# Key and query numbers of an attention layer as rows in two parts, in a four-layer graph network on one core

## The chip, the cores and the metric

The kernel runs on one core of one Trainium2 chip. Its time is the device time of one execution in microseconds (us), the median of several. A core has five engines that work side by side, each through its own queue in a fixed order: TensorE (PE) multiplies matrices, VectorE (DVE), ScalarE (ACT) and GpSimd (POOL) work on elements, SyncE (SP) issues transfers. They wait for each other by semaphores: an instruction that waits holds up all that stands behind it in its queue.

## The reference, cut to what matters

For each of 16 graphs (512 nodes, 128 numbers per node) four layers follow one another, each on `relu(layernorm(x))`, each with a residual. Layer 0 is where the numbers of the change are used:

```python
feat_proj = (feats @ fc_w + fc_b)            # 8 heads of 128
q = feat_proj @ q_w + q_b                    # one number per node and head
k = feat_proj @ k_w + k_b
logits = q + swapaxes(k, -1, -2)             # 512 x 512 per head
attn = softmax(leaky_relu(logits + (1 - adj) * NEG))
out = sigmoid((attn @ feat_proj).reshape(...) @ fp_w + fp_b + feats)
```

Layer 1 is an attention by `h A h'` with a gate, layer 2 five steps of aggregation and a GRU cell, layer 3 a convolution of 17 taps, distance weights and one more GRU cell.

## The kernel before, in words

Two slots hold two graphs at a time; buffers end in 0 or 1. While graph g goes through softmax (ACT, DVE, POOL) the graph before it goes through layers 2 and 3 (mostly PE), so PE has work of two graphs mixed together. Who comes when is not found by the hardware but written down: every engine's work is cut into steps of strands (`values`, `keys`, `heads`, `layer1`, ...), a table `TURN` gives each step a time and `START` one to each graph, and `in_order` issues the steps by that sum. Changing the numbers changes the fixed order of a queue, and nothing else.

Matrices with full precision are kept as a high and a low part (type fp32r): `mm3` (lines 508, 509, 512) adds high x high, low x high and high x low. Where a weight of 128 x 128 meets 512 columns, this is three instructions.

The places of the change. `values` on PE (line 586 and around) turns the normalized rows of a graph over (`transpose_in`, line 562), then takes 16 numbers per node, the 8 query and 8 key numbers, by 12 products of 16 columns with `VQH` and `VQL` (bank 3), and then eight times `mm3` for the heads' values (the first of each 12 with the weight `M`). Ahead of the 12 stand five products whose result nobody reads (line 586). DVE adds the biases (`QK`, line 1171) and scales (`QN`, line 1174). `keys` on PE (line 619) needs the key numbers of one head as a row repeated on all 128 partitions: four transposes of a broadcast column of `QK`. DVE's masking (line 1201) adds adjacency, ACT exponentiates (lines 908 and 914) with its sums in `den`, DVE inverts them (`rden`, line 1213), POOL scales (line 445), PE turns tiles over (line 638) and multiplies them with the values (line 644), DVE and ACT copying the turned tiles (lines 1223 and 926).

In the same stretch DVE serves layer 1 of the other graph: dots for the gate (line 1256), the new `X` (line 1312), its statistics (lines 1118 to 1126), `AN` from the adjacency (line 1320), and the normalized rows `hN` (line 1132), which PE turns over before layer 2 begins (line 562, then `HT`, line 728, and the aggregation, lines 741 and 745). A GRU cell ends with DVE's lines 1350 and 1352; `accY` is the one of layer 3. Layer 1's sum over neighbours is line 711, the end of a graph on PE line 569.

Of the kernel before, what the change touches and what calls it, by code (L numbers as in the profile page):

```python
# [28 lines left out]
for _name, _width in WIDTHS:  # L29
# [7 lines left out]
AUG = 32 * (BLOCKS - 1) + ROWS5  # L37

# [4 lines left out]
        "bse", "scm", "scs", "hcm", "hcs", "hbm", "hbs", "bmsg"] + ["nq%d" % c for c in range(AUG)] + ["gw%d" % c for c in range(2 * DIM)])  # L43
# [10 lines left out]
    "mask0": 1, "qk_banked": 1, "qk": 1, "g_banked": 8, "g_act": 4, "g_dve": 4,  # L54
# [28 lines left out]
START = (0.000, 130.369, 260.718, 391.050, 521.380, 651.749, 782.086, 912.423, 1042.760,  # L83
          1173.097, 1303.435, 1433.772, 1564.109, 1694.446, 1824.783, 1955.120)
# [3 lines left out]
    ("SP", "transfers"): (3515.678, 3562.397, 3562.397, 3575.622, 3634.067, 3711.988),  # L88
    ("Pool", "inputs"): (3230.966, 3241.946, 3349.882),
    ("Pool", "normalized"): (3291.779, 3291.779, 3291.779, 3291.779, 3291.779, 3291.779, 3293.808, 3298.303,  # L90
# [31 lines left out]
    ("Activation", "values"): (3320.761, 3330.097, 3334.275, 3344.175, 3345.848),  # L122
# [61 lines left out]
def build(nc, x, adj, adjt, nmask, c2w, wraw, prew, fcw, fpw, cols_d, out):  # L184
    with ExitStack() as ctx:
# [7 lines left out]

        WH = sb("WH", [P, WALL], F32R)
        WLO = sb("WLO", [P, WALL], F32R)
        VQH = sb("VQH", [P, 2 * HEADS], F32R)
        VQL = sb("VQL", [P, 2 * HEADS], F32R)
        VQ = sb("VQ", [P, 2 * HEADS])
        CQ = sb("CQ", [P, 2 * HEADS])
# [300 lines left out]
        def _(pe):  # L500
# [71 lines left out]
            def values(g):  # L572
# [930 lines left out]
```

## Time and profile before

| what | us |
|---|---|
| median of 3 runs | 2175.18 |
| lowest and highest run | 2172.43, 2176.92 |
| the profiled execution | 2177.26 |
| its span, first to last instruction | 2175.2 |
| PE busy | 2061.6 (95%) |
| DVE, ACT, POOL busy | 1609.2, 1517.9, 777.0 |

The profile is of one execution; about 2.1 us lie outside its span. A PE instruction's shown duration includes its way through the array: the next starts before it ends. How long one holds the engine is therefore read from one start to the next. TensorE's clock has two levels, 1.2 and 2.4 GHz; PEclk 1.00 in a row means 2.4 GHz throughout, 0.50 means 1.2 GHz throughout.

### The profile page before, as it was taken

The numbers are of one execution on the slowest core, as the hardware profiler recorded it, in microseconds if no ns is written. First come the engines' busy times: TensorE is split into PE (matmuls) and PEld (weight loads), VectorE is DVE, ScalarE is ACT, GpSimd is POOL, SyncE is SP. The second block draws the span as 40 slices with busy tenths as digits, with TensorE's granted clock in tenths as the row PEclk, the third lists the DMA queues.
The fourth block names the chain that finished last, engine by engine and source line by source line (L and its number), as shares of the span: only waits on it lengthen the run. The fifth ranks groups of instructions, "written<-read, shape, count | busy, mean of one in ns | idle before, by whom it ended". The sixth has DMA issues, their size and how long they took to land. (4 is left out here: it accounts for less than half of the span.)

```text
span 2175.2 us, 36465 instructions
## 1 busy us (share of the span) xinstructions
PE 2061.6 (95%) x12700; PEld 1748.4 (80%) x12700; DVE 1609.2 (74%) x4782; ACT 1517.9 (70%) x2968; POOL 777.0 (36%) x888
## 2 busy tenths in 40 slices
PE   7799999999999999999999999999999999999876
PEld 6678797887978878797887979888797888879754
DVE  5687887868778687887868778686877868788643
ACT  5677594967849677694967859587694967859432
POOL 2334334242423433333343433434243342433311
PEclk9999999999999999999999999999999999999988
DMA  3101001010100101001010100101001010100100
GB/s 120 49 20 45 25 1 44 26 45 25 45 25 2 44 25 45 25 2 50 19 45 25 45 25 2 44 25 45 25 28 42 1 44 25 45 6 1 49 0 5
DMA packets 47319, 65.73 MB, mean 30 GB/s; under 512 B 3744, under 2 KB 21536, under 8 KB 47008
## 3 DMA queue, kind: packets, MB, share of 16 engines
q1 hardware_dynamic: 47136, 63.41, 8.9%
q8 instruction: 100, 1.64, 0.3%
q14 instruction: 83, 0.68, 0.1%
HBM read 59.21 MB, written 4.19 MB: 29 GB/s over the span
## 5 line engine op out<-in xcount | busy, mean ns | idle before, releaser
L644 PE MATMUL banks<-F,PT 128*128 128x128 f32 x4096 | 543.3, 276 | 2.3 <-DVE PT L1223 1.5
L644 PEld LDWEIGHTS banks<-F,PT 128*128 128x128 f32 x4096 | 507.1, 192 | 15.2 <-DVE PT L1223 2.0
L478 POOL TENSOR_TENSOR HS<-HT,HS 128x512 fp32r<-128x512 f32 x64 | 83.4, 1304 | 539.4 <-ACT HS L990 539.4
L1223 DVE COPY PT<-banks 128x512 f32<-128x512 f32 x256 | 175.7, 686 | 116.2 <-PE banks L638 115.5
L926 ACT ACTIVATE PT<-banks 128x512 f32<-128x512 f32 x256 | 151.2, 591 | 89.0 <-PE banks L638 87.1
L961 ACT ACTIVATE F<-banks,dcols 128x512 f32<-128x512 f32 x288 | 193.6, 684 | 23.3 <-PE banks L512 19.1
L445 POOL TENSOR_SCALAR tiles<-tiles,rden 128x512 f32<-128x512 f32 x192 | 143.7, 763 | 97.1 <-DVE rden L1213 96.9
L415 POOL TENSOR_TENSOR rstd<-var,mhalf 128x4 f32<-128x4 f32 x64 | 72.4, 1131 | 271.4 <-DVE var L1126 271.4
L508 PE MATMUL banks<-HS,WH 128*128 128x512 f32 (+1 forms) x368 | 157.9, 429 | 1.6 <-ACT HS L889 1.4
L445 POOL TENSOR_SCALAR U<-U,rden 128x512 f32<-128x512 f32 x192 | 130.5, 699 | 72.7 <-DVE rden L1213 72.5
L509 PE MATMUL banks<-HS,WLO 128*128 128x512 f32 (+1 forms) x368 | 147.5, 401 | 0.0
L914 ACT ACTIVATE tiles<-tiles 128x512 f32<-128x512 f32 x192 | 138.5, 721 | 9.1
L914 ACT ACTIVATE U<-U 128x512 f32<-128x512 f32 x192 | 138.6, 722 | 5.4 <-DVE rden L1213 0.4
L445 POOL TENSOR_SCALAR adjT<-adjT,rden 128x512 f32<-128x512 f32 x128 | 88.2, 699 | 140.8 <-DVE rden L1213 140.7
L908 ACT ACTIVATE U<-U,QN 128x513 f32<-128x513 f32 x192 | 137.3, 715 | 1.4 <-DVE U L1201 1.4
L908 ACT ACTIVATE tiles<-tiles,QN 128x513 f32<-128x513 f32 x192 | 137.5, 716 | 0.0
L508 PE MATMUL banks<-R,WH 128*128 128x512 f32 x336 | 135.2, 402 | 1.4 <-DVE R L1412 1.4
L509 PE MATMUL banks<-R,WLO 128*128 128x512 f32 x336 | 133.1, 396 | 0.0
L512 PE MATMUL banks<-R,WH 128*128 128x512 f32 x336 | 132.0, 400 | 0.0
L512 PE MATMUL banks<-HS,WH 128*128 128x512 f32 (+1 forms) x368 | 129.6, 401 | 0.0
L1201 DVE CUSTOM_DVE_ANT_0 U<-adjN,banks 128x512 f32<-128x512 f32 x192 | 124.4, 679 | 0.6 <-issue 0.6
L1201 DVE CUSTOM_DVE_ANT_0 tiles<-adjN,banks 128x512 f32<-128x512 f32 x192 | 124.4, 679 | 0.0
(216 smaller groups left out, 5309.3 us busy)
## 6 DMA issues: line engine op xcount, KB each, us to landing
adjN<-in_adj_dram SPq DMA_DIRECT2D x32, 1024.0 KB, 5.6
adjT<-in_adjt_dram SPq DMA_DIRECT2D x16, 1024.0 KB, 5.7
xin<-in_x_dram SPq DMA_DIRECT2D x18, 256.0 KB, 2.9
out_dram<-X SPq DMA_DIRECT2D x16, 256.0 KB, 6.0
F<-in_wraw_dram SPq DMA_DIRECT2D x1, 1076.0 KB, 9.6
adjT<-in_c2w_dram SPq DMA_DIRECT2D x1, 1024.0 KB, 11.1
PT<-in_fcw_dram SPq DMA_DIRECT2D x1, 512.0 KB, 5.2
PT<-in_fpw_dram SPq DMA_DIRECT2D x1, 512.0 KB, 6.8
```

Source lines behind the costliest of these rows:

```text
L445: pool.tensor_scalar(SC[s][h % RING][:, t, 0:NODES], SC[s][h % RING][:, t, 0:NODES], rden[s][:, t:t + 1], 1.0, ALU.mult, ALU.mult).then_in ...
L478: pool.tensor_tensor(HL[s], HT[s][:, :], HH[s].bitcast(F32), ALU.subtract).then_inc(S["h_new_low"], 1)
L508: pe.matmul(dst, w[0], xs[0], start=start, stop=False)
L509: pe.matmul(dst, w[1], xs[0], start=False, stop=False)
L512: return pe.matmul(dst, w[0], xs[1], start=False, stop=stop)
L644: last = pe.matmul(B[s][:, 3, part(j)], PT[s][:, k, part(j)], G[s][:, k, h * DIM:(h + 1) * DIM], start=(h == 0 and j == 0 and k == 0), sto ...
L908: act.activation(SC[s][h % RING][:, t, :], SC[s][h % RING][:, t, :], ACT.Prelu, bias=QN[s][:, t, h:h + 1], scale=0.01, alpha=100.0).then_i ...
L914: act.activation(SC[s][h % RING][:, t, 0:NODES], SC[s][h % RING][:, t, 0:NODES], ACT.Exp, bias=SC[s][h % RING][:, t, NODES:NODES + 1], sca ...
L926: act.activation(PT[s][:, j, :], pt_bank(s, j), ACT.Copy).then_inc(S["pt_act"], 1)
L961: act.activation(F[s][:, tile, :], B[s][:, bank, :], func, bias=dcol(bias), scale=0.5)\
L1201: dve.tensor_tensor_reduce(out=SC[s][h % RING][:, t, 0:NODES], in0=adjN[s][:, t, :], in1=B[s][:, 0, :], scale=1.0, scalar=3.0e38, op0=ALU. ...
L1223: dve.tensor_copy(PT[s][:, j, :], pt_bank(s, j)).then_inc(S["pt_dve"], 1)
```

## The change

The query and key numbers are computed the other way round: the stationary side is now `VQH` and `VQL` with 104 columns, so that three products of 512 columns give rows (partitions 0 to 7 and 32 to 39 the keys, 64 to 71 and 96 to 103 the queries, each twice). ACT writes the high part of one copy (`KS`, for the other copy zero, by a scale column of 0 or 1), DVE subtracts it from the bank: `KR` then holds high and low part of each row, as fp32r, in partitions of their own. One product of a column of `pick` (0 and 1) broadcast to 128 columns with `KR` adds both parts and puts one head's key row on all partitions; four small products with `pick` give back the query numbers per node. `den` and `rden` get three sets. Waits that others imply are dropped. Five unread products become 17, in another place, for every graph but the first; there are 18 in the first graph's layer 1, and, for the last graph only, 26, five times 10, 13 and 13. The bias row `ob` is computed earlier at the start. `START` and the whole of `TURN` are other numbers.

```diff
-START = (0.000, 130.369, 260.718, 391.050, 521.380, ...
+START = (0.000, 131.658, 263.298, 394.959, 526.603, ...
-    ("PE", "keys"): (3288.100, 3289.199, 3290.522, 3298.667, 3321.282, 3343.182, 3360.968, 3375.271),
+    ("PE", "keys"): (166.698, 169.779, 177.359, 190.668, 191.962, 214.493, 223.487, 236.182),
...
+        KS = [U[s][0:ROWSQ, TILES - 1, :].bitcast(F32R) for s in SL]
-        den = [sb(f"den{s}", [P, TILES]) for s in SL]
+        den = [sb(f"den{s}", [P, RING, TILES]) for s in SL]
...
-                pe.matmul(B[1][:, 3, 0:HEADS], dcol("qkw").broadcast_to([P, P]), cols[:, 0:HEADS]).then_inc(vq_banked, 1)
+                pe.matmul(B[1][:, 3, 0:HEADS], dcol("qkw").broadcast_to([P, P]), cols[:, 0:HEADS])
+                for h in range(HEADS):
+                    pe.matmul(B[1][:, 3, P:2 * P], cols[:, h:h + 1].broadcast_to([P, P]), fp[:, part(h)], start=(h == 0), stop=False)
+                pe.matmul(B[1][:, 3, P:2 * P], col("fpb").broadcast_to([P, P]), ident[:, :], start=False, stop=True)\
+                    .then_inc(vq_banked, 1)
...
+            def busy(bank, n):
+                for k in range(n):
+                    pe.matmul(bank, WH[:, 0:P], WH[:, 0:4 * P])
...
-                if g >= SLOTS:
-                    for k in range(5):
-                        pe.matmul(B[s][:, 3, :], WH[:, 0:P], WH[:, 0:4 * P])
-                pe.wait_ge(*own("h_low", g, 0))
                 if g == 0:
                     pe.wait_ge(vq_low, 1)
-                for t in range(TILES):
-                    last = mm3(B[s][:, 3, 16 * t:16 * t + 16], (HH[s][:, part(t)], HL[s][:, part(t)]),
-                               (VQH[:, :], VQL[:, :]))
+                pe.wait_ge(*own("h_high", g, 0))
+                high(B[s][0:ROWSQ, 3, :], (VQH[:, :], VQL[:, :]), (HH[s], HL[s]))
+                pe.wait_ge(*own("h_low", g, 0))
+                low(B[s][0:ROWSQ, 3, :], (VQH[:, :], VQL[:, :]), (HH[s], HL[s])).then_inc(S["kq_banked"], 1)
+                yield
+                if g >= 1:
+                    busy(B[s][:, 0, :], 17)
+                pe.wait_ge(*after("kq_rows", g))
+                for t in range(TILES):
+                    last = pe.matmul(B[s][:, 0, HEADS * t:HEADS * (t + 1)], KR[s][64:ROWSQ, part(t)], pick[64:ROWSQ, :])
                 last.then_inc(S["qk_banked"], 1)
...
-                    if i == 2:
-                        pe.wait_ge(*after("qk", g))
...
-                    for t in range(TILES):
-                        last = pe.transpose(B[s][:, 0, part(t)],
-                                            QK[s][:, t, HEADS + h:HEADS + h + 1].broadcast_to([P, P]), ident[:, :])
-                    last.then_inc(S["kb_banked"], 1)
+                    pe.matmul(B[s][:, 0, :], pick[0:32 + HEADS, h:h + 1].broadcast_to([32 + HEADS, P]),
+                              KR[s][0:32 + HEADS, :]).then_inc(S["kb_banked"], 1)
...
+                    busy(B[s][:, 1, :], 18)
...
+                if g == GRAPHS - 1:
+                    busy(B[s][:, 1, :], 26)
...
+                        if g == GRAPHS - 1:
+                            pe.wait_ge(*after("r", cell - 1))
+                            busy(B[s][:, 2, :], 10)
...
+                if g == GRAPHS - 1:
+                    pe.wait_ge(*after("c2_scaled", g))
+                    busy(B[s][:, 3, :], 13)
                 pe.wait_ge(*after("nmp_low", g))
...
+                act.wait_ge(*after("kq_banked", g))
+                act.activation(KS[s], B[s][0:ROWSQ, 3, :], ACT.Identity, bias=0.0, scale=cols[0:ROWSQ, CI["qlow"]:CI["qlow"] + 1])\
+                    .then_inc(S["kq_high"], 1)
...
+                dve.wait_ge(*after("kq_high", g))
+                dve.tensor_tensor(KR[s][:, :], B[s][0:ROWSQ, 3, :], KS[s].bitcast(F32), ALU.subtract).then_inc(S["kq_rows"], 1)
```

Three places show what this does to a queue. In these rows `[waits ...]` names the semaphores, and L numbers are the lines of the kernel that the rows belong to (before: 569 graph's end, 586 unread products; after: 572 the same end, 558 unread products, 598 the query numbers).

PE before, where a graph ends (`accY`) and the values of the next in that slot begin:

```order
L569 MATMUL banks0<-ident,accY0 128x128 [waits h_new]
L569 MATMUL banks0<-ident,accY0 128x128 x3
L586 MATMUL banks0<-WH 128x512 [waits hn]
L586 MATMUL banks0<-WH 128x512 x4
L508 MATMUL banks0<-VQH,HS0 128x16 [waits h_low_0]
L509 MATMUL banks0<-VQH,HS0 128x16
L512 MATMUL banks0<-VQL,HS0 128x16
```

PE after, the same place:

```order
L508 MATMUL banks0<-HS0,VQH 104x512 [waits h_high_0,hn]
L509 MATMUL banks0<-HS0,VQL 104x512
L512 MATMUL banks0<-HS0,VQH 104x512 [waits h_low_0]
L572 MATMUL banks0<-ident,accY0 128x128 [waits h_new]
L572 MATMUL banks0<-ident,accY0 128x128 x3
L558 MATMUL banks0<-WH 128x512 x17
L598 MATMUL banks0<-pick,KR0 128x8 [waits kq_rows]
L598 MATMUL banks0<-pick,KR0 128x8 x3
L508 MATMUL banks0<-WH,HS0 128x512 [waits h_new]
```

The three row products moved ahead of the graph's end, and all value products now stand behind `kq_rows`.

DVE before, serving this place (slot 1 begins, slot 0 ends its layer 1; `var`, `AN`, `hN` belong to layer 1 and 2):

```order
L1126 TENSOR_SCALAR var0<-mv0 128x4 [waits aggregated_0]
L1171 TENSOR_TENSOR QK1<-banks1,CQ 128x64 [waits qk_banked]
L1174 TENSOR_SCALAR QN1<-QK1 128x32 [waits qk]
L1320 TENSOR_SCALAR AN0<-adjN0 128x2048 [waits hp_banked,adjN_loaded0]
L1132 TENSOR_SCALAR hN0<-X0,mv0,rstd0 128x128 [waits rstd_0]
L1132 TENSOR_SCALAR hN0<-X0,mv0,rstd0 128x128 x3
```

DVE after (1192 is the new subtraction, 1169 the residual that before stood ahead of the gate dots):

```order
L1138 TENSOR_SCALAR var0<-mv0 128x4 [waits aggregated_0]
L1192 TENSOR_TENSOR KR1<-banks1,U1 104x512 [waits kq_high]
L1169 TENSOR_TENSOR X1<-banks1,X1 128x512 [waits y_banked_1]
L1335 TENSOR_SCALAR AN0<-adjN0 128x2048 [waits hp_banked,adjN_loaded0]
L1144 TENSOR_SCALAR hN0<-X0,mv0,rstd0 128x128 [waits rstd_0]
L1144 TENSOR_SCALAR hN0<-X0,mv0,rstd0 128x128 x3
L1195 TENSOR_TENSOR QK1<-banks1,CQ 128x32 [waits qk_banked]
```

`KR` took the place of `QK`, which moved behind `hN`; the residual moved from ahead of the gate to here.

PE after, between two cells of the last graph's layer 2 (before, the transposes of line 728 followed the last product at once):

```order
L512 MATMUL banks1<-R1,WH 128x512
L558 MATMUL banks1<-WH 128x512 [waits r]
L558 MATMUL banks1<-WH 128x512 x9
L730 MATMUL banks1<-ident,HT1 128x128 [waits h_new]
L730 MATMUL banks1<-ident,HT1 128x128 x3
```

Ten unread products now stand in what was a bare wait for `h_new`.

## Rows read from the trace of the kernel before

**Rows 1.** Page, part 1: busy time, share, instructions
```profile
PE 2061.6 (95%) x12700; PEld 1748.4 (80%) x12700; DVE 1609.2 (74%) x4782; ACT 1517.9 (70%) x2968; POOL 777.0 (36%) x888
```

**Rows 2.** Timeline of DVE: start us, us, engine, line, what; one QK per graph
```profile
20.99 0.22 DVE L1171 TENSOR_TENSOR QK<-banks,CQ 128x64 f32<-128x64 f32 x1 [0.76 <-PE banks L512]
...
119.14 0.22 DVE L1171 TENSOR_TENSOR QK<-banks,CQ 128x64 f32<-128x64 f32 x1
...
1935.85 0.22 DVE L1171 TENSOR_TENSOR QK<-banks,CQ 128x64 f32<-128x64 f32 x1
```

**Rows 3.** Waits of PE from 249 to 1936 us: total us, times, longest
```profile
PE banks L508 <- DVE QK L1171: 21.3, 13, 1.9
PE banks L728 <- ACT HT L954: 8.5, 13, 0.7
PE banks L569 <- DVE accY L1352: 3.3, 13, 0.3
...
PE banks L728 <- DVE HT L1352: 1.4, 7, 0.5
```

**Rows 4.** Timeline of PE: two products of 512 columns, then two groups of transposes
```profile
909.63 0.39 PE L508 MATMUL banks<-WH,HS 128*128 128x512 f32 x1
909.86 0.39 PE L509 MATMUL banks<-WH,HS 128*128 128x512 f32 x1
...
952.86 0.60 PE L619 MATMUL banks<-ident,QK 128*128 128x128 f32 x4
953.30 0.60 PE L638 MATMUL banks<-ident,U 128*128 128x128 f32 x4
```

**Rows 5.** Timeline of PE where one graph ends and the next begins
```profile
1022.16 0.66 PE L569 MATMUL banks<-ident,accY 128*128 128x128 f32 x4 [0.26 <-DVE accY L1352]
1022.57 1.40 PE L586 MATMUL banks<-WH 128*128 128x512 f32 x5
1024.20 0.28 PE L508 MATMUL banks<-VQH,HS 128*128 128x16 f32 x1 [0.23 <-DVE HS L1138]
...
1028.81 0.50 PE L508 MATMUL banks<-WH,HS 128*128 128x512 f32 x1 [1.63 <-DVE QK L1171]
...
1032.36 0.66 PE L728 MATMUL banks<-ident,HT 128*128 128x128 f32 x4 [0.69 <-ACT HT L954]
```

**Rows 6.** Timeline of DVE in the same stretch
```profile
1021.41 0.69 DVE L1352 SCALAR_TENSOR_TENSOR accY<-F 128x512 f32<-128x512 f32 x1
1022.85 0.69 DVE L1157 TENSOR_TENSOR X<-banks,X 128x512 f32<-128x512 f32 x1 [0.75 <-PE banks L569]
1023.46 0.68 DVE L1138 SCALAR_TENSOR_TENSOR HS<-banks,HS 128x512 fp32r<-128x512 f32 x1
...
1028.45 0.17 DVE L1126 TENSOR_SCALAR var<-mv 128x4 f32<-128x4 f32 x1
...
1028.88 1.22 DVE L1320 TENSOR_SCALAR AN<-adjN 128x2048 fp32r<-128x2048 f32 x1
1030.17 1.11 DVE L1132 TENSOR_SCALAR hN<-X,mv,rstd 128x128 f32<-128x128 f32 x4
```

**Rows 7.** Stretches: us, busy PE, PEld, DVE, ACT, POOL, clock, DMA share, GB/s
```profile
249.30:378.90 129.60, 126.63 (x790) 107.81 (x790) 99.76 (x298) 94.26 (x185) 48.46 (x55) 1.00 0.09 29
...
2080.90:2091.30 10.40, 7.02 (x30) 5.15 (x30) 5.09 (x9) 4.50 (x7) 1.30 (x1) 1.00 0.01 2
...
2115.00:2127.60 12.60, 9.20 (x30) 7.06 (x30) 5.09 (x8) 4.50 (x7) 1.29 (x1) 0.77 0.00 0
2127.60:2145.00 17.40, 12.07 (x40) 8.38 (x40) 5.08 (x22) 3.77 (x6) 2.98 (x3) 0.62 0.00 1
```

**Rows 8.** Timeline of PE with the last graph alone
```profile
2080.99 0.66 PE L728 MATMUL banks<-ident,HT 128*128 128x128 f32 x4 [3.37 <-DVE HT L1352]
...
2135.47 0.63 PE L509 MATMUL banks<-HS,WLO 128*128 128x512 f32 x1
2135.90 0.63 PE L508 MATMUL banks<-HS,WH 128*128 128x512 f32 x1
```

More of the change, by code:

```diff
@@ L42 @@
         "bih3r", "bih3z", "bih3n", "bhh3r", "bhh3z", "bhh3n",
-        "bse", "scm", "scs", "hcm", "hcs", "hbm", "hbs", "bmsg"] + ["nq%d" % c for c in range(AUG)] + ["gw%d" % c for c in range(2 * DIM)])
+        "qlow", "bse", "scm", "scs", "hcm", "hcs", "hbm", "hbs", "bmsg"] + ["nq%d" % c for c in range(AUG)] + ["gw%d" % c for c in range(2 * DIM)] + ["pk%d" % h for h in range(HEADS)])
 CI = {n: i for i, n in enumerate(COLS)}
@@ new lines @@
+    ("SP", "transfers"): (0.000, 6.720, 28.455, 31.853, 211.238, 217.728),
+    ("Pool", "inputs"): (63.748, 71.077, 175.343),
+    ("Pool", "normalized"): (137.764, 137.764, 140.756, 140.756, 145.791, 145.958, 146.520, 146.641, 148.247,
[26 rows of a table added]
+    ("Activation", "values"): (280.268, 283.534, 283.534, 289.782, 308.796, 312.315),
+    ("Activation", "weights"): (281.986, 281.986, 287.195, 307.884, 309.784),
+    ("Activation", "softmax"): (294.464, 295.181, 295.181, 298.237, 303.387, 309.676, 309.676, 311.233, 311.233,
[5 rows of a table added]
@@ new lines @@
+    ("Activation", "tile_copies"): (314.345, 318.415, 328.588, 332.960, 346.050, 351.163, 352.673, 357.805, 362.988,
[9 rows of a table added]
+    ("DVE", "values"): (291.932, 299.290, 303.284, 311.648, 312.505, 316.050, 316.827, 319.568, 320.672, 321.279),
+    ("DVE", "weights"): (300.169, 306.745, 311.878, 313.915, 313.915, 320.273, 320.273, 351.308),
+    ("DVE", "softmax"): (317.554, 317.711, 318.421, 318.503, 320.486, 321.059, 321.500, 321.500, 330.265, 330.265,
+        338.773, 343.405, 359.012, 367.293, 367.342, 367.342, 379.728, 381.734, 387.576, 390.185, 391.958, 392.222,
+        393.928, 394.317, 398.780, 401.731, 404.237, 404.237, 415.564, 421.165, 423.967, 424.135),
@@ L234, in build @@
         HT = [sb(f"HT{s}", [P, NODES]) for s in SL]
-        hN = [sb(f"hN{s}", [P, NODES]) for s in SL]
+        hN, KR = [], []
+        for s in SL:
+            with nc.sbuf_tensor(f"hN{s}", [P, NODES], F32) as t:
+                hN.append(t)
+            KR.append(sb(f"KR{s}", [ROWSQ, NODES], F32R))
         X = [sb(f"X{s}", [P, TILES, DIM]) for s in SL]
@@ L238, in build @@
         nm = [sb(f"nm{s}", [P, TILES]) for s in SL]
-        QK = [sb(f"QK{s}", [P, TILES, 2 * HEADS]) for s in SL]
+        QK = [sb(f"QK{s}", [P, TILES, HEADS]) for s in SL]
         QN = [sb(f"QN{s}", [P, TILES, HEADS]) for s in SL]
@@ L536, in weights @@
                 last.then_inc(m_banked, 1)
-                yield
-                pe.wait_ge(vq_ready, 1)
-                for h in range(HEADS):
-                    pe.matmul(B[1][:, 3, 0:DIM], cols[:, h:h + 1].broadcast_to([P, P]), fp[:, part(h)], start=(h == 0), stop=False)
-                pe.matmul(B[1][:, 3, 0:DIM], col("fpb").broadcast_to([P, P]), ident[:, :], start=False, stop=True)\
-                    .then_inc(m_banked, 1)
                 yield
@@ L666, in scores @@
                     if t == 0:
-                        pe.wait_ge(*after("t1_high", g))
                         pe.wait_ge(*after("h1_high", g))
@@ L707, in layer1 @@
                     yield
-                    pe.wait_ge(*after("h1_scaled", g, t + 1))
+                    if t % 2 == 0:
+                        pe.wait_ge(*after("h1_scaled", g, t + 1))
                     pe.wait_ge(*attended(g, t))
@@ L738, in layer2 @@
                     pe.wait_ge(*after("rows_high", turn))
-                    pe.wait_ge(*after("adjacency", g))
+                    if layer == 0:
+                        pe.wait_ge(*after("adjacency", g))
                     for t in range(TILES):
@@ L772, in layer3 @@
                 yield
+                if g == GRAPHS - 1:
+                    pe.wait_ge(*after("r", cell - 1))
+                    busy(B[s][:, 2, :], 10)
                 pe.wait_ge(*after("h_new", cell - 1))
@@ L775, in layer3 @@
                 yield
+                if g == GRAPHS - 1:
+                    busy(B[s][:, 2, :], 13)
                 transpose_in(g, 3)
@@ L778, in layer3 @@
                 pe.wait_ge(*own("h_high", g, 3))
-                pe.wait_ge(*own("residual", g, 2))
                 high(B[s][:, 1, :], W("c1"), (HH[s], HL[s]))
@@ L1072, in weights @@
                 vq = B[1][:, 2, 0:2 * HEADS].rearrange("p (h a) -> p a h", a=2)
[L1073 to L1075 removed]
+                dve.tensor_scalar(CQ[:, :], B[1][:, 3, 0:HEADS], d2("tq"), None, ALU.add)
+                for a in (0, 32):
+                    dve.tensor_scalar(VQ[:, a:a + HEADS], vq[:, 1, :], -1.0, None, ALU.mult)
+                dve.tensor_copy(pick[:, :], cols[0:ROWSQ, CI["pk0"]:CI["pk0"] + HEADS])
+                for a in (64, 96):
+                    last = dve.tensor_copy(VQ[:, a:a + HEADS], vq[:, 0, :])
+                last.then_inc(vq_ready, 1)
+                dve.tensor_copy(ob[:, :], B[1][:, 3, P:2 * P]).then_inc(ob_ready, 1)
                 yield
@@ L1210, in denominators @@
                         dve.wait_ge(*after("exped", g * HEADS + h, t + 1))
-                        if h >= 1:
-                            dve.wait_ge(*after("attn", g * HEADS + h - 1, t + 1))
-                        dve.reciprocal(rden[s][:, t:t + 1], den[s][:, t:t + 1]).then_inc(S["rden"], 1)
+                        dve.reciprocal(rden[s][:, h % RING, t:t + 1], den[s][:, h % RING, t:t + 1]).then_inc(S["rden"], 1)
             def tile_copies(g):
@@ L1327, in cand_a @@
                 s = g % SLOTS
-                dve.wait_ge(*after("hn", cell))
-                dve.wait_ge(*after("r", cell))
+                dve.wait_ge(*after("r" if cell % (LAYERS2 + 1) < LAYERS2 else "hn", cell))
                 dve.scalar_tensor_tensor(F[s][:, 3, :], F[s][:, 0, :], 1.0, F[s][:, 2, :], ALU.add, ALU.mult)\
@@ L1472, in rows @@
         return _np.array(values, _np.float32)
-    none = rows(0, 0, 0, 0, 0)
+    none, heads_one = rows(0, 0, 0, 0, 0), _np.ones(HEADS, _np.float32)
     moving, still = rows(1, 1, 1, 0, 1), rows(2, 2, 2, 1, 0)
     moving_one, still_one = rows(0, 0, 0, -1, 0), rows(0, 0, 0, 0, -1)
-    nq = _np.zeros((P, AUG), _np.float32)
+    nq, pick = _np.zeros((P, AUG), _np.float32), _np.tile(_np.eye(32, HEADS, dtype=_np.float32), (4, 1))
     for b in range(BLOCKS):
```

107 lines of the change are left out of this document (43 added, 64 removed), and 102 rows, old and new, of the table TURN.

## The prediction, made before the changed kernel ran

> **What bounds the kernel now.** I read the busy times first: PE is busy for 2061.6 us of 2175.2 [rows 1], everything else much less. Then the rhythm: DVE's `QK` comes once per graph, from 119.14 to 1935.85 in 14 equal steps of 129.8 us [rows 2], so those 1817 us are one pattern; before it stand 21 us of setup and 98 us with one graph, behind it 239 us in which the last graph ends up alone. In a steady step the clock is 1.00 and PE is idle for about 3 of 129.6 us [rows 7]. The list of waits says where: `QK` 21.3 us in 13 graphs (1.6 each), `HT` from ACT 8.5, `accY` 3.3, and `HT` from DVE 1.4 [rows 3]. The first three are one place, the border between two graphs [rows 5]. Outside it PE hardly waits, so there a product taken off PE is time gained, and a product put on is time lost; at the border the chain through DVE decides. The last 115 us are different: PE waits 3.4 us in each cell [rows 8], and the granted clock falls.
>
> **The keys of a head.** One product of 512 columns holds PE for 0.23 us (909.63 to 909.86), a group of four transposes for 0.44 (952.86 to 953.30) [rows 4]. The change puts one of the former for one of the latter, eight times a graph, which is 0.21 us each. The first is part of the border, below. The second stands right ahead of a cell's `HT`, for which PE already waits in 7 of 13 graphs [rows 3], so what it frees is waited away. Six remain: 6 x 0.21 = 1.27 us a graph. The product has 40 rows and a broadcast weight, a form that no row shows. Bounds: as dear as four transposes (0) and, with all eight counted, 1.7 us. I take 1.27, since its 512 columns are those of the neighbouring products.
>
> **The border, PE's work.** Twelve small products go (about 0.11 each, the rate of the transposes: 1.3 us), and five unread ones (1.2 us). Three row products (0.7), four small ones (0.4) and 17 unread ones (17 x 0.23 = 3.95 us) come. Together with the keys that is 6.1 us off PE (with all 32 transposes) and 7.0 us on: PE's total work per graph grows by 0.9 us. Whether the kernel gets faster hangs on the 3.95 us lying inside a wait.
>
> **The border, the chain.** I walk it on the clock of [rows 5, 6]. `accY` is ready at about 22.1 (times less 1000). Before: DVE idles until PE has turned it over, adds the residual at 22.85, and starts `HS` at 23.46; `var` starts 5.0 us later at 28.45, then `QK`, `AN` at 28.88, `hN` at 30.17, ready at 31.28, and PE begins with `HT` 1.1 us after that at 32.36. After: `HS` is next to `accY` and starts at 22.1; the same run of gate, `X` and statistics is then over at 27.2; `KR` (one more pass of 512, 0.61 as between 22.85 and 23.46) to 27.85; the residual, moved here, to 28.45; `AN` 1.3 to 29.75; `hN` ready at 30.8. So `HT` on PE starts at 31.9 instead of 32.36. ACT has one extra copy to `KS` ahead and one copy of a value more between `HT` and the rows of the cell, so of these 0.45 us I keep 0.3.
> On PE: the third row product waits for `HS` until 22.8, and ends at 23.05; the transposes of `accY` end at 23.5, the 17 unread products at 27.4. `KR` is there at 27.9. They lie inside the wait, with 0.5 us left bare. Then four small products to 28.35, nine value products to 30.45, and PE waits again for `hN` at 30.8. What lies behind `KR` on PE, all value products of the graph, has the slack of that last wait (0.35 us) and no more. What hides the 17 products is DVE's gate and statistics of the other graph; if that cover went, each would cost 0.23 us. Bounds of the border: 1.0 us gained (if all waits but `hN`'s closed) and 2.8 us lost (twelve more unread products wholly on top). I take 0.3 gained, as the walk uses durations of the very same instructions.
>
> **The new order.** Nearly all steps got other times. I compared the queues of PE, DVE and ACT over one graph. Between a cell's last product and the next cell's transposes there stands as much softmax work as before or more, and a row of masks ahead of a cell's subtraction is matched by PE work put in the same gap. The cover over layer 1's normalization and over layer 3's `nmp_low` is thinner, by about 1 us and 0.3 us, but by the durations still enough. I take off 0.06 for this. Dropped waits and the three sets of `den` cost and give nothing where PE is the bound: they are implied by others, and ACT is 27% idle [rows 7].
> Per graph: 1.27 + 0.3 - 0.06 = 1.5 us. Fourteen steps [rows 2]: 21.0 us. The last graph's softmax, beside the layers of the one before, has the same keys again: 1.3.
>
> **The end.** From 2067 us on one graph runs alone. A cell at clock 1.00 takes 10.40 us, one at 0.77 takes 12.60, though all instructions are the same [rows 7]. A product of 512 columns holds PE for 0.43 us at the lower level (2135.47 to 2135.90) [rows 8] instead of 0.23. Three of the four cells behind the first are slow, the longest by 2.2 us, which bounds them at 6.6; the start of layer 3 runs at 0.62 [rows 7], and nine such products and eight transposes there, at most twice as long, give 3 us more; some 0.5 more at the very end. The change fills these waits: ten unread products are 2.3 us in a wait of 3.4 plus the products' tail [rows 8], 26 are 6.1 us ahead of `hN`, where PE idles for some 7. If that holds the level at 2.4 GHz, up to 10 us come back. I take 8; bounds 0 and 10. They cost something where they outlast the wait: the last 13 hold PE for 3.0 us, and the row they stand before is ready earlier than that, which I put at 0.3 within the 8. Should all of them run at the lower level, 26 x 0.43 = 11.2 us, and up to 4 us would be lost there.
>
> **The start.** `QK` of the first graph comes at 20.99 [rows 2]. Ahead of it now lie an ACT pass, a DVE pass and the bias products, some 3 us by the same lengths. Against that, ACT, which bounds the first graph's softmax, gets the big conversion of weights before it instead of within it, and 18 unread products should keep the clock up in layer 1. I take 1 us gained, between 3 lost and 3 gained.
>
> **The sum.** 21.0 + 1.3 + 8 + 1 = 31.3 us off the profiled execution of 2177.3 (span 2175.2) is 2146.0. That execution is 2.1 above the median of the runs, so the forecast is 2143.9 us.
>
> **Rivals.**
> *The unread products lie on top* (slower). Suppose rows, gate and statistics don't stretch over the 17 products, or the new order leaves as much waiting as there was: 129.6 us a graph plus the 0.9 of work. Then 14 x 0.9 = 12.6 and 0.8 for the last softmax are lost; with 9 gained at both ends it ends at 2179.6 from a base of 2175.2, and with the ends at zero at 2189. It decides from about 2.1 us more idle time a graph than I found. For it: PE's work does grow, and every value product now depends on one row of DVE that has a long queue ahead. Against it: the walk above, on DVE's own rows [rows 6].
> *The clock at the end does not hold.* Then the 8 are missing: 2152. Speaking for it: waits of more than 1 us remain in each cell even with ten products in them. Against: in the steady stretch waits of 1.6 and 0.7 us leave it at 1.00 [rows 5, 7]. The Trainium skill, "TensorE: Matmul & The Clock Gate", section "A second HAM failure mode: psum-queue depth-cycling", says that frequent short idles between groups of products can make the clock swing between its levels; by that rule this rival holds, and the steady stretch here speaks against it.
> *The key product is no cheaper* than four transposes (the change doesn't do what it says): 1.27 x 14 + 1.3 = 19 us less gain, 2163.
> *The order is better than I can see*: PE's remaining waits close as well, 1.3 us a graph more, 2125.
>
> **Chances.** Forecast 0.56; clock 0.12, 2152; key product 0.08, 2163; on top 0.17, 2180; better order 0.07, 2125. The range runs from 2127 to 2176: it takes in the bounds of the border and the keys except for the far end of the slower rival and half of the best. A change of 0.2% (4.35 us) is about what a measurement of this kernel can tell from none, so faster is below 2170.8, slower above 2179.5. All cases but the slower rival are faster, which gives 0.80 with a rest for their tails; the rival straddles the upper bound: same 0.09, slower 0.11.
>
> **What would show each step.** In the new profile: steps between two `QK` of 128.3 us; the key product 0.23 us from its start to the next; the 17 products followed by a wait of about 0.5 us for `KR`; `HT` on PE about 9.8 us after `accY` instead of 10.2; no new entry of over 0.3 us a graph in the list of PE's waits; cells of the last graph near 10.4 us at clock 1.00. A step of 130.5 us would be the slower rival. I would be wrong most easily in the new order: a wait for `weights3`, `normed` or `masked` in the middle of a graph, which the queues alone don't show, would cost its length 14 times.

## The result: slower by 42 us, and the profile after

The changed kernel takes 2217.1 us (median of 4 runs, 2213.2 to 2219.3), the kernel before 2174.7 in the same company: a ratio of 1.0192, 95% interval 1.0179 to 1.0204. The forecast was 2143.9. The profiled execution of the changed kernel is one of 2213.2 us (span 2211.4); the forecast for such a one was 2146.0, so 67 us are to be explained.

The rhythm tells most of it. These are the first two and the last `QK` on DVE, from the order of time of the changed kernel (columns: start, duration, engine, line, operation, output<-input, shape):

```profile
25.22 0.18 DVE L1195 TENSOR_TENSOR QK<-banks,CQ 128x32 f32<-128x32 f32 x1
...
127.08 0.18 DVE L1195 TENSOR_TENSOR QK<-banks,CQ 128x32 f32<-128x32 f32 x1
...
1980.17 0.18 DVE L1195 TENSOR_TENSOR QK<-banks,CQ 128x32 f32<-128x32 f32 x1
```

The 14 steps behind 127.08 are 132.36 us long, 2.6 more than in [rows 2] and 4.1 more than forecast: 57 of the 67 us. The second `QK` comes 7.9 us later than before, where 1 us earlier was forecast: 9 more. Behind the last one the kernel takes 231.2 us instead of 239.4, 8.2 less, where 9.3 was forecast.

The list of PE's waits in the steady stretch, 260 to 1975 us, has become shorter than [rows 3]:

```profile
PE banks L598 <- DVE KR L1192: 17.9, 12, 1.5
PE banks L572 <- DVE accY L1366: 2.8, 11, 0.3
PE banks L508 <- DVE X L1169: 1.9, 1, 1.9
PE banks L512 <- DVE HS L1150: 0.8, 2, 0.4
```

About 1.9 us a graph instead of 2.9, all at the border. So in each graph PE is busy for 3.6 us more than before, where the forecast has 0.9 more work. A busy PE is not PE at its peak: what is missing stands in the distances from start to start. Two places show it. The first is a key product between two groups of transposes and value products, PE in the order of time:

```profile
443.45 0.60 PE L636 MATMUL banks<-ident,U 128*128 128x128 f32 x4
443.98 0.50 PE L622 MATMUL banks<-KR,pick 40*128 40x512 f32 x1
444.41 1.16 PE L642 MATMUL banks<-F,PT 128*128 128x128 f32 x8
445.40 0.60 PE L636 MATMUL banks<-ident,U 128*128 128x128 f32 x4
```

Four transposes hold PE until 443.98, which is 0.53 instead of the 0.44 of [rows 4]; the key product 0.43 instead of 0.23; the eight value products behind it 0.99 instead of 0.89. From 443.45 to 445.40 are 1.95 us. In the kernel before the same stretch, with four transposes for the key product, took 0.44 + 0.44 + 0.89 = 1.77. The product of 512 columns is dearer than the four transposes, by 0.18 us. It is not the product alone (0.43 against their 0.44): its neighbours are held longer too.

The second place is the border between two graphs, here one with its clock below it (columns of the windows: the stretch, its length, busy us and number of PE, PEld, DVE, ACT, POOL, then the granted clock, DMA share, GB/s):

```profile
647.09 0.60 PE L572 MATMUL banks<-ident,accY 128*128 128x128 f32 x4
647.45 4.13 PE L558 MATMUL banks<-WH 128*128 128x512 f32 x17
652.92 0.60 PE L598 MATMUL banks<-pick,KR 40*128 40x8 f32 x4 [1.35 <-DVE KR L1192]
...
654.00 0.63 PE L509 MATMUL banks<-WH,HS 128*128 128x512 f32 x1
654.43 0.63 PE L512 MATMUL banks<-WLO,HS 128*128 128x512 f32 x1
...
656.98 0.40 PE L512 MATMUL banks<-WLO,HS 128*128 128x512 f32 x1
657.21 0.60 PE L565 MATMUL banks<-ident,hN 128*128 128x128 f32 x4
```

```profile
649.00:652.90 3.90, 2.57 (x12) 1.80 (x10) 3.69 (x17) 0.82 (x2) 0.55 (x1) 1.00 0.00 0
...
654.00:657.00 3.00, 3.00 (x9) 2.32 (x8) 2.53 (x8) 0.60 (x1) 0.00 (x0) 0.51 0.39 85
657.00:660.00 3.00, 3.00 (x17) 2.24 (x16) 1.69 (x7) 2.12 (x4) 0.00 (x0) 1.00 0.97 317
```

Behind the 17 unread products PE stands still for 1.35 us, not the 0.5 of the forecast, and then the granted clock is 0.51, the level of 1.2 GHz: the value products are 0.43 us apart instead of 0.23. This happens at 9 of the 14 borders. By the granted clock of the trace, TensorE is at the lower level for 35 us of the 14 steps, all of it at borders, against 7 us in the kernel before.

Why `KR` is late stands on DVE. The same border one graph earlier, DVE and the one pass of POOL that falls in it:

```profile
514.21 0.69 DVE L1366 SCALAR_TENSOR_TENSOR accY<-F 128x512 f32<-128x512 f32 x1
514.82 0.68 DVE L1150 SCALAR_TENSOR_TENSOR HS<-banks,HS 128x512 fp32r<-128x512 f32 x1
515.42 0.28 DVE L1271 CUSTOM_DVE_ANT_0 F<-F,cols 128x128 f32<-128x128 f32 x1
...
515.62 1.37 DVE L1271 CUSTOM_DVE_ANT_0 F<-F,cols 128x128 f32<-128x128 f32 x1
...
516.93 0.28 DVE L1271 CUSTOM_DVE_ANT_0 F<-F,cols 128x128 f32<-128x128 f32 x1
...
520.98 0.68 DVE L1192 TENSOR_TENSOR KR<-banks,U 104x512 fp32r<-104x512 f32 x1
```

```profile
515.47 1.37 POOL L469 TENSOR_TENSOR F<-F 128x512 f32<-128x512 f32 x1 [5.50 <-ACT F L958]
```

One of the four gate sums (the dots for the gate) takes 1.37 us; its sisters take 0.28. It ends 0.1 us after POOL's pass. This is so at each of the 14 borders. In [rows 6] `HS` stood behind the residual, 1.4 us later, and the gate sums began at 1024.06, when POOL's pass was over. In the kernel before that pass is this one:

```profile
1022.68 1.30 POOL L469 TENSOR_TENSOR F<-F 128x512 f32<-128x512 f32 x1 [5.06 <-ACT F L948]
```

One border of the 14, called the odd one below, is unlike the others, and unlike the queues shown ahead of the prediction: there the residual (L1169) stands on DVE behind `AN` and `hN` instead of ahead of them. Their due times in `TURN` are 578.279 and 446.661, 131.618 apart; the starts of neighbouring graphs are 131.640 or more apart, but for one pair with 131.611, and there the order turns round. PE's value products wait for it; that is the one wait of 1.9 us for `X` in the list above.

### The profile page after: what moved, and what is told of

Same layout as the page of the kernel before. It is cut to its first block and busy times, and to the rows that moved or that the text cites. A ratio compares the mean times of both kernels' runs of the same rounds, so it can differ in the third digit from the quotient of the medians.

```text
span 2211.4 us, 34516 instructions
## 1 busy us (share of the span) xinstructions
PE 2140.0 (97%) x12541; PEld 1768.7 (80%) x12541; DVE 1641.2 (74%) x4801; ACT 1511.3 (68%) x2984; POOL 798.8 (36%) x888
## 5 line engine op out<-in xcount | busy, mean ns | idle before, releaser
L445 POOL TENSOR_SCALAR U<-U,rden 128x512 f32<-128x512 f32 x192 | 140.4, 743 | 369.7 <-DVE rden L1230 368.6
L936 ACT ACTIVATE PT<-banks 128x512 f32<-128x512 f32 x256 | 150.6, 588 | 96.8 <-PE banks L636 96.4
L445 POOL TENSOR_SCALAR tiles<-tiles,rden 128x512 f32<-128x512 f32 x192 | 138.0, 726 | 90.7 <-DVE rden L1230 89.3
L508 PE MATMUL banks<-HS,WH 128*128 128x512 f32 (+1 forms) x368 | 155.3, 422 | 1.4 <-ACT HS L899 1.4
L445 POOL TENSOR_SCALAR adjT<-adjT,rden 128x512 f32<-128x512 f32 x128 | 93.5, 741 | 127.5 <-DVE rden L1230 127.5
L512 PE MATMUL banks<-HS,WH 128*128 128x512 f32 (+1 forms) x368 | 127.5, 396 | 0.0
```

Source lines behind the costliest of these rows:

```text
L445: pool.tensor_scalar(SC[s][h % RING][:, t, 0:NODES], SC[s][h % RING][:, t, 0:NODES], rden[s][:, h % RING, t:t + 1], 1.0, ALU.mult, ALU.mul ...
L508: pe.matmul(dst, w[0], xs[0], start=start, stop=False)
L512: return pe.matmul(dst, w[0], xs[1], start=False, stop=stop)
L936: act.activation(PT[s][:, j, :], pt_bank(s, j), ACT.Copy).then_inc(S["pt_act"], 1)
```

## The experiments

Each has the changed kernel as its base unless it says otherwise. "Step" is the mean of the 14 steps between `QK`s; the ratios are to the kernel before on the same chip. The last column is the time in these 14 steps for which the granted clock is at 1.2 GHz, idle time of PE included.

| kernel | us | ratio, 95% interval | step | us at 1.2 GHz in 14 steps |
|---|---|---|---|---|
| before | 2174.7 | 1 | 129.8 | 7 |
| changed | 2217.1 | 1.0192 (1.0179 to 1.0204) | 132.4 | 35 |
| e1_wide | 2173.4 | 0.9993 (0.9984 to 1.0002) | 129.8 | 22 |
| e9_rows64 | 2211.3 | 1.0167 (1.0146 to 1.0189) | 132.3 | 36 |
| e5_free | 2189.8 | 1.0067 (1.0050 to 1.0084) | 130.8 | 3 |
| e2_busy0 | 2228.4 | 1.0244 (1.0229 to 1.0259) | 133.5 | 101 |
| e8_busy23 | 2198.0 | 1.0113 (1.0094 to 1.0132) | 131.3 | 0 |
| e6_wide_free | 2151.5 | 0.9900 (0.9884 to 0.9916) | 128.6 | 3 |
| e7_kr_first | 2148.9 | 0.9888 (0.9872 to 0.9905) | 128.4 | 0 |
| e12_no13 | 2147.5 | 0.9881 (0.9867 to 0.9896) | 128.5 | 3 |
| e10_an_pool | 2222.3 | 1.0223 (1.0208 to 1.0238) | 133.1 | 61 |
| e11_less | 2223.7 | 1.0233 (1.0216 to 1.0250) | 133.1 | 82 |
| e4_tail (on before) | 2171.7 | 0.9983 (0.9974 to 0.9993) | 129.7 | 3 |
| e13_order (on before) | 2221.0 | 1.0211 (1.0193 to 1.0228) | 132.7 | 89 |

**e1_wide: the rows of the key product.**

```
-pe.matmul(B[s][:, 0, :], pick[0:32 + HEADS, h:h + 1].broadcast_to([32 + HEADS, P]), KR[s][0:32 + HEADS, :])
+pe.matmul(B[s][:, 0, :], pick[:, h:h + 1].broadcast_to([ROWSQ, P]), KR[s][:, :])
```

`pick` gets a second set of columns, for the query products, which take all rows too; the set for the keys is zero in the rows of the queries, and the other way round.

> The changed kernel, with the key product and the four small query products taking all 104 rows of `KR` (the rows that are not wanted meet zeros in `pick`) instead of 40. Theory: the 40-row product holds PE for 0.43 us because of its row count, and what stands next to it is held 0.1 us longer too; with 104 rows it takes 0.23 as its neighbours do. Then a graph's step falls by 8 x 0.2 = 1.6 us, up to 2.0, from 132.4 to about 130.6, and the time from 2217 to about 2193. Rival: the broadcast weights are what costs (or the change between a product of this kind and one of transposes): then it stays at 0.43 and the time at 2217.

The theory held, and more came than the 1.6 to 2.0 us a graph that it asked for: 2.6. The same place in its trace:

```profile
428.59 0.60 PE L636 MATMUL banks<-ident,U 128*128 128x128 f32 x4
428.95 0.48 PE L622 MATMUL banks<-KR,pick 104*128 104x512 f32 x1
429.26 1.05 PE L642 MATMUL banks<-F,PT 128*128 128x128 f32 x8
430.15 0.60 PE L636 MATMUL banks<-ident,U 128*128 128x128 f32 x4
```

0.36, 0.31 and 0.89: 1.56 us, 0.39 less than with 40 rows and 0.21 less than the 1.77 of the transposes, which is the very difference that the forecast took. Eight times 0.39 are 3.1; 2.6 arrive, and a little of these may be clock (22 us at the lower level instead of 35). That the rest is lost in PE's waits at the border is likely and was not taken apart. The broadcast weights are still there, so it isn't they.

**e9_rows64: 64 rows instead of 104.**

```
-pe.matmul(..., pick[:, h:h + 1].broadcast_to([ROWSQ, P]), KR[s][:, :])
+pe.matmul(..., pick[0:64, h:h + 1].broadcast_to([64, P]), KR[s][0:64, :])
```

> As the first experiment (104 rows), but the key product takes 64 rows of `KR`; the query products stay at 104. Tells what it is about the 40 rows. If products with few rows are dear because their rows are not those of the products around them, 64 rows should cost like 40: 0.53, 0.42 and 0.34 us from start to start before, at and behind the key product, and about 2.5 us a graph more than with 104 rows, 2209. If only a count that is no multiple of 32, or one that splits a group of rows, is dear, 64 costs like 104 and the time is 2173.

64 rows cost what 40 do (0.53, 0.42 and 1.00 from start to start in the same kind of place, the median of 28), so it is neither a count that is no multiple of 32 nor one that splits a group. A product that uses half of the rows or fewer, among products that use more, is what is dear, and what stands on either side of it pays too. Tried were 40, 64 and 104 rows. The Trainium skill has a rule that would explain it, "TensorEngine Tiling (Array Packing)", sections "Tiling Modes", "Key Properties" and "When to Use Tiling": arrays of 64 rows, for 64 contraction rows or fewer, are a mode of their own, and changing the mode drains the engine. It presents the mode as something one chooses. That a plain product of few rows falls into it is an inference; no trace shows the mode. The price agrees in kind: 0.39 us for a key product and its two changes.

**e5_free: POOL's pass away from the gate sums.** X = (h - hp) gate + (x + h + hp) is written (h - hp)(gate - 1) + (x + 2h):

```
-pool.wait_ge(*after("hp", g))
-pool.tensor_tensor(F[s][:, 7, :], F[s][:, 6, :], F[s][:, 2, :], ALU.add)
+pool.tensor_tensor(F[s][:, 7, :], F[s][:, 6, :], F[s][:, 5, :], ALU.add)
...
+dve.tensor_scalar(gate[s][:, 0, :], gate[s][:, 0, :], -1.0, None, ALU.add).then_inc(S["gate_less"], 1)
+dve.wait_ge(*after("gate_less", g))
```

> The changed kernel, with X = (h - hp)(gate - 1) + (x + 2h) in place of (h - hp) gate + (x + h + hp): GpSimd's pass that waited for hp now needs only h, and runs some 6 us earlier, away from DVE's gate sums; DVE gets one pass of 4 columns more. Theory: GpSimd's pass and DVE's gate sums hold each other up at the border (one pass of 128 columns takes 1.37 us there and 0.28 elsewhere). Then that pass takes 0.28, `KR` comes 0.9 us earlier, PE's wait for it falls from 1.5 to 0.6, the step by 0.9, and by up to 1.9 if the clock no longer falls behind the wait: 2204 to 2190. Rival: the long pass has another cause: it stays at 1.37 and the time at 2217 or a little above.

Held, at the good end. All four sums now take 0.28, and `KR` comes 5.7 us after the start of `accY` at every border instead of 6.8. Two of the four:

```profile
507.80 0.28 DVE L1270 CUSTOM_DVE_ANT_0 F<-F,cols 128x128 f32<-128x128 f32 x1
...
508.00 0.29 DVE L1270 CUSTOM_DVE_ANT_0 F<-F,cols 128x128 f32<-128x128 f32 x1
```

PE waits 0.5 for `KR` instead of 1.5 (and 0.7 instead of 0.3 for `accY`), and the clock falls at one border only: the odd one, where PE also waits 2.3 us for the residual. 27 us in all.

**e2_busy0 and e8_busy23: the number of unread products at the border.** 0 and 23 instead of 17:

```
-busy(B[s][:, 0, :], 17)
+busy(B[s][:, 0, :], 23)
```

> The changed kernel without the 17 unread products at the border between two graphs. Theory: DVE's chain to `KR` sets the border, the products lie inside PE's wait; then PE waits 5.5 us there instead of 1.5, the step stays at 132.4, and the time within 6 us of 2217 (the clock may fall for longer behind the longer wait: up to 2 us a graph more, 2245). Rival, the one put on record as slower: the products lie on top: then 3.95 us a graph come back, a step of 128.5 and 2162 us.

> The changed kernel with 23 unread products at the border instead of 17. Six more are 1.4 us, which is the wait for `KR` (1.5 us). Theory: the clock falls only because PE stands still there for 1.5 us; with the wait filled it stays at its upper level, the 35 us at the lower level in 14 graphs go, half of them are time: a step about 1.2 us shorter, 2200. Rival: the fall has nothing to do with the wait, or more products outlast it: 2217 or more.

Both theories held. Without the 17, not one of their 3.95 us comes back: PE waits 5.4 us in every graph, and the clock falls in each such wait or right behind it.

```profile
PE banks L596 <- DVE KR L1190: 64.4, 12, 5.4
```

The step becomes 1.1 us longer, not shorter, so the rival of the record, unread products on top, is out. With 23 the wait is closed and the clock stays at its upper level through all 14 steps (columns as in the windows above; the clock is the 1.00):

```profile
124.72:1962.38 1837.66, 1829.29 (x10905) 1519.43 (x10905) 1424.81 (x4173) 1311.83 (x2604) 694.63 (x770) 1.00 0.09 29
```

The step is 1.1 us shorter although PE has 1.4 us more to do. That is the price of the wait of 1.5 us, as clock and not as idle time: 35 us at half speed are at most 17.5 us of work, 1.2 us a graph, and 1.1 come back.

**e6_wide_free: both edits.**

> The changed kernel with both edits: key and query products over 104 rows, and GpSimd's pass no longer behind hp. Theory: the two losses are separate things in separate places, so they add: from a step of 132.4 the 2.6 us of the one and the 1.6 of the other go, 128.2, with at most 0.5 shared, since each of the two has part of its gain from the same low clock behind the wait for `KR`; 2217 - 44 - 27 = 2146, up to 2152. Rival: the border and the keys share one limit (DVE's chain): then the second edit brings less than half of its 27, and the time is over 2160.

They add: 2151.5 us where the sum said 2146 to 2152. The mean step is 128.6, and 12 of the 14 lie within 0.2 of 128.3, which is the forecast's own number. The other two are 129.3 and 131.4, on both sides of the odd border, where PE waits for the residual and the clock falls behind the wait:

```profile
763.61 0.80 PE L507 MATMUL banks<-WH,HS 128*128 128x512 f32 x1 [2.35 <-DVE X L1168]
```

These 4.1 us are the whole difference of 0.3 us a graph. The parts of the forecast that no experiment names apart (the new order elsewhere, the walk along DVE without the stall) so hold as a sum; their errors may cancel, since the keys alone now save 8 x 0.21 = 1.7 us where 1.27 was forecast, and PE waits 0.7 us for `accY` instead of 0.3. The kernel is 1.0% faster than the one before.

**e7_kr_first: `KR` ahead of the statistics.** One due time of the statistics on DVE is raised from 443.857 to 444.500, so that `KR` comes first.

> As the last one, with `KR` on DVE ahead of the statistics instead of behind them. Theory: with the stall gone, `hN` (statistics, reciprocal root on GpSimd, `AN` in between) is what PE waits for last, and `KR` 0.6 us earlier only moves PE's wait from the small query products to the transposes of `hN`: the step stays within 0.2 us, the time within 3 us of the last one. Rival: `KR` sets the border: a step 0.4 to 0.6 us shorter, 6 to 8 us in all.

As expected: PE's wait for `KR` is gone, the transposes of `hN` are now what comes last (four of them take 0.82 us from start to start, each held back a little, instead of 0.35), the step is 0.2 us shorter. In this kernel DVE works without a gap from `accY` to `hN`, so its passes should set the border; the next experiment was to show it and did not get that far.

**e10_an_pool and e11_less: `AN` on POOL, then fewer unread products** (base: e6_wide_free).

```
-dve.tensor_scalar(AN[s][:, :, :], adjN[s][:, :, :], 0.0, None, ALU.not_equal)
+pool.tensor_scalar(AN[s][:, :, :], adjN[s][:, :, :], 0.0, None, ALU.is_gt)
```

> As the kernel with both edits (104 rows, GpSimd's pass freed), and the pass that writes `AN` (2048 columns, 1.1 us of DVE) goes to GpSimd, which is idle there (with `greater than 0` for `not 0`, the same for entries 0 and 1). Theory: with the stall gone DVE works without a gap from `accY` to `hN`, so its passes set the border; 1.1 us fewer give `hN` up to 0.9 us earlier (GpSimd's reciprocal root then comes last), but with 17 unread products PE is behind by itself: some 0.3 to 0.5 us a graph, 2144 to 2147. Rival: GpSimd's long pass and DVE's gate sums hold each other up as the other pass did: one gate pass of 2 us, and 10 us or more lost, 2162.

> As the last one, with 12 unread products at the border instead of 17 (1.17 us less of PE's work). Theory: there the unread products are on top by now; the step falls by up to 0.9 us against the kernel with both edits, 2138. Rival 1: DVE still sets the border: PE waits longer, the time stays within 3 us of the last one. Rival 2 (if GpSimd's pass stalls DVE): within 3 us of the last one too, but with the wait for `KR` of over 2 us in the list.

The rival won by far. POOL needs 5.76 us where DVE took 1.22, and the first gate sum waits for most of it:

```profile
511.12 3.13 DVE L1274 CUSTOM_DVE_ANT_0 F<-F,cols 128x128 f32<-128x128 f32 x1
```

```profile
510.08 5.76 POOL L471 TENSOR_SCALAR AN<-adjN 128x2048 fp32r<-128x2048 f32 x1 [3.22 <-PE banks L711]
```

The next sum starts at 514.18, while POOL's pass ends at 515.84 in the profile, in which the spans of POOL are rough: here DVE seems not to wait for its end, unlike at L469. PE then waits 3.3 us for `KR`. The second kernel lost as much, as its second rival says: less work on PE can't help where DVE is late. Part of the 4.5 us a graph that are lost is the clock again, 61 us at the lower level.

**e13_order: the order alone, on the kernel before.** One due time: the last graph's residual (L1157) moves from between `accY` and `HS` to behind `QK` and `QN`.

> The kernel before with one step of the new order alone: on DVE the last graph's residual no longer stands between `accY` and `HS`, but behind the statistics. Theory: the order alone makes the stall. `HS` comes 1.4 us earlier, the gate sums then fall on GpSimd's pass and one of them takes 1.37 us instead of 0.28; that and the residual behind the statistics eat the gain: `hN` within 0.3 us of where it was, the step within 0.3, the time between 2172 and 2178. Rival: no stall without the rest of the change: `hN` 0.9 us earlier, a step of 128.9, and 2162.

The mechanism held and the time did not: 2221.0, 47 us slower. The stall is there (one gate sum of 1.38 at 1039.70), and `hN` starts 9.0 us after `accY` instead of 8.8. But my expectation left out that PE's second value product waits for this residual, and what the clock makes of that:

```profile
1046.14 0.80 PE L508 MATMUL banks<-WH,HS 128*128 128x512 f32 x1 [3.27 <-DVE X L1157]
1046.73 0.63 PE L509 MATMUL banks<-WH,HS 128*128 128x512 f32 x1
...
1050.15 1.05 PE L619 MATMUL banks<-ident,QK 128*128 128x128 f32 x4
...
1052.74 0.66 PE L728 MATMUL banks<-ident,HT 128*128 128x128 f32 x4 [0.69 <-ACT HT L954]
```

The wait is 3.27 us instead of 1.63 [rows 5] and comes three products earlier. The nine products behind it take 4.0 us, which at 0.23 each would be 2.1, and the transposes behind them twice their time, all on the way to `HT`, which comes 14.5 us after the start of `accY` instead of 10.95. The clock in this stretch:

```profile
1046.10:1050.20 4.10, 4.06 (x10) 3.10 (x11) 2.83 (x6) 0.60 (x1) 1.16 (x1) 0.50 0.39 82
```

Over the 14 steps it is at the lower level for 89 us instead of 7, after each of the 14 waits. One moved step of DVE, 0.61 us long, costs more than the whole change, most of it by way of the clock behind a wait that is 1.6 us longer. It also shows that the stall needs nothing but the order; its own price here stands inside the 47 us and was not taken apart.

**e4_tail and e12_no13: the unread products of the last graph.** The first adds them (26, 10 a cell, 13, 13) to the kernel before. The second takes the last 13 out of e7_kr_first:

```
-if g == GRAPHS - 1:
-    pe.wait_ge(*after("c2_scaled", g))
-    busy(B[s][:, 3, :], 13)
```

> The kernel before, with only the unread products of the last graph added (26 ahead of `hN` in layer 1, 10 in each wait of a cell, 13 and 13 in layer 3). Theory: they hold the clock at its upper level there, which is worth 8 us: 2167. Rival: the part of the changed kernel behind the last `QK` is 8 us shorter for another reason (its keys, its order): 2175.

> As the kernel with `KR` ahead of the statistics, without the 13 unread products ahead of `nmp_low` in the last graph. Theory: they outlast their wait: from the transposes of layer 3 to those of `accY` the last graph takes 28.7 us with them and 27.6 in the kernel before, at the same clock. Without them 1.1 us less, 2148. Rival: they keep the clock up there: without them it falls, and the time is 1 to 3 us longer.

They hold the clock: in e4_tail the granted clock stays at its upper level from 2072.7, in the first cell, until the last 5 us of the kernel, and the cells of the last graph come 10.4 us apart, as the one cell at clock 1.00 did in the kernel before [rows 7]:

```profile
2080.50 0.66 PE L737 MATMUL banks<-ident,HT 128*128 128x128 f32 x4 [1.08 <-DVE HT L1369]
2090.89 0.66 PE L737 MATMUL banks<-ident,HT 128*128 128x128 f32 x4 [1.06 <-DVE HT L1369]
2101.28 0.66 PE L737 MATMUL banks<-ident,HT 128*128 128x128 f32 x4 [1.08 <-DVE HT L1369]
2111.69 0.66 PE L737 MATMUL banks<-ident,HT 128*128 128x128 f32 x4 [1.06 <-DVE HT L1369]
```

But the gain is 3.3 us by the medians (4.6 from the first `HT` of the last graph to its `accY` in the traces), not 8. The last 13 are part of the reason: from the transposes of layer 3 (L790 before, L797 after) to those of `accY` it takes 27.6 us before, 28.7 in the changed kernel and 30.0 in e4_tail. Without them 2147.5 instead of 2148.9; the intervals of the two overlap, so the medians alone don't settle it, and the traces show 27.1 us in that stretch instead of the 28.7 of e7_kr_first: 1.5 less. This is the fastest kernel here, 1.2% ahead of the one before.

## Why the prediction was wrong, step by step

**The keys of a head: the step that failed first.** "I take 1.27, since its 512 columns are those of the neighbouring products": the columns are, the 40 rows are not. The term was bounded by "as dear as four transposes (0)", and the product is dearer than they are: 0.18 us more instead of 0.21 less, eight times a graph. The text had named the form as one that no row shows and then bounded it by rows of other forms, with no room for a loss. e1_wide gives 2.6 us a graph back, and 5.0 us in the first graph, where the next `QK` comes 96.8 us after the first instead of 101.9. In all 42 of the 67 us, profile against profile (44 by the medians). The rival "the key product is no cheaper" (2163) had the place right and ended its price at zero.

**The border, the chain: right walk, one pass overlooked.** The walk used durations of the same instructions and moved them 1.4 us earlier. It didn't ask what other engines do at the new time. POOL's pass behind hp, 1.3 us long, starts 1.3 us after `accY` in both kernels; the gate sums came to lie on it. The forecast has `KR` on DVE 5.8 us after the start of `accY`; it came after 6.8. So the wait of 0.5 us became 1.5. e5_free takes it away. The Trainium skill says it of this pair of engines, "SBUF — State Buffer", section "Who interferes with whom": a DVE instruction with two inputs in SBUF contends with a GpSimd instruction that reads there; one with a single input, outside the modes of DVE that take two ports, does not. The traces agree: the gate sums read `F` and `cols`, and wait; the residual pass of [rows 6], with one input in the banks, ran from 1022.85 beside the same pass of POOL (from 1022.68, 1.30 us) and took its 0.61 us.

**The border, PE's work: right.** The 17 products lie inside the wait, with 1.5 us bare instead of 0.5; nothing comes back without them (e2_busy0).

**What the forecast had no term for: the clock inside the steady stretch.** It cited waits of 1.6 and 0.7 us at clock 1.00 [rows 5, 7] against the rival of the clock at the end, and didn't ask whether a wait behind other neighbours would leave it there. It does not: 1.35 to 1.5 us behind 17 products let it fall in 9 of 14 graphs. The rule of the Trainium skill that is cited there is about frequent short idles between groups of products. The middle has one such wait a graph, so it is hardly that case; the end with its ten products in each cell comes nearer to it, and there the clock stayed up behind waits of 1.1 us. What decides between a fall and none behind 1.5 us, the runs don't show. e8_busy23 prices the falls at 1.1 us a graph; part of what e5_free gains is the same money.

**The new order: right but for one border.** No wait of over 0.3 us a graph appeared in the middle, and e6_wide_free runs at the forecast step. The place at which I said I would most easily be wrong was not the place. The queues were compared over one graph, though, and at one border of the 14 they differ: `X` behind `hN`, 4.1 us in e6_wide_free, 0.3 a graph. `START` and `TURN` alone would have told it.

**The end: right in direction, too high.** 8.2 us came in all where 9.3 was forecast. The cells came out as forecast, 10.4 us at clock 1.00, and that is 5 of the 8; the last 13 products cost 1.1 to 1.5 instead of 0.3. In e4_tail the products alone bring 3.3 to 4.6 us. Where the rest of the 8.2 comes from was not taken apart.

**The start: wrong, by 4 us beside the rows.** `QK` comes at 25.2 instead of 21.0, and of the gain that was set against it nothing shows. (In e2_busy0 and e8_busy23, whose start is the same code, it comes at 23.5 and 23.8, so up to 1.7 us of the 4.2 may belong to this one execution.) The bias products for `ob` now hold PE for 3.6 us (from 12.86) ahead of the product of the weights, where before they came behind it; so ACT's conversion of `WH` begins at 20.14 instead of 16.66. DVE's part of the weights' split waits 1.5 us for that, `KR` (22.34) stands behind it, and the small products wait 2.3 us for `KR`. The better pace after e1_wide pays 1.3 of the 4.2 back. This was read from the trace and not tried.

The sum: 57 us in the steps (2.6 a graph for the rows; 1.2 more that came with POOL's pass and the clock behind the wait; 0.3 from the odd border), 9 at the start (5 of them the rows again), 1 at the end.

## What to carry to other kernels

A product of few rows among products of many was not priced by its columns here: give it the rows of its neighbours, with zeros where it has none, before counting what it saves. When a change moves an engine's passes in time, look at what the other engines do at the new time, above all GpSimd under any pass of DVE with two inputs in SBUF. And of a wait on PE ask not only how long it is but what stands behind it: products at half the clock on the chain can cost more than the wait, and filling it with unread products was worth 1.1 us a graph here. A fixed order that is right for one graph has to be looked at for all of them.

## What the runs showed of the hardware that I had not expected

- A product with 40 or 64 rows and 512 columns held PE for 0.43 us where one with 104 rows took 0.31 in the same place, and its neighbours lost 0.17 ahead and 0.10 behind (e1_wide, e9_rows64).
- A gate sum of DVE, 0.28 us, waited out GpSimd's pass of 1.37 us; beside one of 5.76 us it took 3.06 us, from 511.12 to 514.18, and was over before that had ended by the profile. GpSimd's pass of 2048 columns took 5.76 us where DVE had 1.22.
- GpSimd suffers too: its reciprocal root of 4 columns took 1.02 us in the changed kernel's border and 2.03 where DVE's pass `AN` fell on it (1045.23 in e13_order).
- At the border a wait of 1.5 us for `KR` was followed by the lower clock in 9 of 14 graphs of the changed kernel and in 7 of 14 of e1_wide, one of 5.4 us in 14 of 14; one of 0.5 us in none but the one where a wait of 2.3 us for the residual came behind it. In the kernel before, with other work around it, a wait of 1.6 us left the clock at 1.00 in 13 of 13, and one of 1.9 us did not. In the last graph of e4_tail waits of 1.1 us in every cell left it at 1.00.
